# Two constant rows added on GpSimd: b2 into x2, be3 into y

## The reference

```python
xp = L_norm @ h                              # 512 x 512, one matrix for all batches
x1 = relu(layernorm(xp @ Wc + bc, g1, be1)) + h
q, k, v = x1 @ Wq, x1 @ Wk, x1 @ Wv          # 4 heads of 32 features
attn = softmax(where(adj > 0, q k^T / sqrt(32), -1e9))
x2 = layernorm(x1 + (attn v) @ Wo + bo, g2, be2)
m = gelu(x2 @ W1 + b1) @ W2 + b2             # the perceptron, 256 hidden features
out = y + layernorm(x2 + m, g3, be3)
```

## Time and profile before

| what | value |
|---|---|
| median of 3 runs | 990.91 us (985.94 to 995.35) |
| the profiled execution | 985.9 us, of it 984.1 us from the first to the last instruction (the span) |
| mean granted TensorE clock | 0.977 |
| PE busy | 910.1 us (92%) in 7110 instructions |
| DVE busy | 613.4 us (62%) |
| ACT busy | 532.6 us (54%) |
| POOL busy | 328.3 us (33%) |
| one full attention round | about 26.4 us |
| after the rounds (915 us to the end) | 69 us |

### The profile page before, as it was taken

One profiled execution on the slowest core, in us unless ns is written; L12 is line 12 of the kernel. 1 busy time (PEld: TensorE's weight loads), 2 busy tenths in 40 slices (PEclk: granted clock), 3 DMA queues, 4 the chain that ended last, 5 costly groups with the idle time before them and its releaser, 6 DMA issues.

```text
span 984.1 us, 20134 instructions
## 1 busy us (share of the span) xinstructions
PE 910.1 (92%) x7110; PEld 748.6 (76%) x7110; DVE 613.4 (62%) x2009; ACT 532.6 (54%) x1178; POOL 328.3 (33%) x426
## 2 busy tenths in 40 slices
PE   5979899999999999989699999999999999888993
PEld 4848799999999999978467777777777777666782
DVE  5842233333333333634588988988888888886786
ACT  3222222222222333220688888888888888885574
POOL 3110011111111111213335545555444544323776
PEclk9988899999999999999799999999999999999998
DMA  3000000000000000004354444455555454410122
GB/s 94 0 1 12 12 11 12 11 11 11 11 11 11 11 11 11 12 1 122 91 130 109 118 108 116 115 129 130 130 131 130 130 127 119 113 32 1 44 65 65
DMA packets 47218, 61.54 MB, mean 63 GB/s; under 512 B 4377, under 2 KB 22050, under 8 KB 47138
## 3 DMA queue, kind: packets, MB, share of 16 engines
q1 hardware_dynamic: 46034, 60.38, 24.1%
q10 hardware_dynamic: 1104, 0.13, 0.1%
HBM read 39.53 MB, written 20.97 MB: 61 GB/s over the span
## 4 chain that ended last, share of the span: by engine, by line
PE 17%; DVE 10%; issue 9%; POOL 9%; ACT 7%; DVEq 0%; POOLq 0%; ACTq 0%
PE bank L1594 5%; PE bank L1614 3%; DVE prob L1764 3%; PE bank L1658 2%; ACT prob L1705 2%; PE bank L1581 2%; POOL z_gain L301 2%; POOL z_norm L305 2%; POOL rstd_b L186 1%; PE bank L333 1%; PE bank L337 1%; POOL x_bo L1538 1%; DVE z_std L282 1%; POOL rstd L186 1%; ACT prob L1377 1%
## 5 line engine op out<-in xcount | busy, mean ns | idle before, releaser
L1705 ACT ACTIVATE prob<-prob,low 128x512 f32<-128x512 f32 x256 | 183.9, 719 | 51.2 <-DVE low L1764 49.4
L1764 DVE CUSTOM_DVE_ANT_0 prob<-bank,mask 128x512 f32<-128x512 f32 x256 | 171.2, 683 | 26.5 <-PE bank L1581 25.4
L1594 PE MATMUL bank<-ident,prob 128*128 128x128 f32 x1024 | 162.8, 282 | 12.3 <-ACT probT L1694 12.2
L1594 PEld LDWEIGHTS bank<-ident,prob 128*128 128x128 f32 x1024 | 114.7, 141 | 58.1 <-issue 30.3
L1581 PE MATMUL bank<-k_stack,q_stack 128*128 128x512 f32 x256 | 123.7, 485 | 8.8 <-PEq L548 4.9
L811 PE MATMUL bank<-B_hi,T_all 128*128 128x384 f32 x384 | 102.3, 340 | 4.6 <-DVE y L1211 2.6
L1694 ACT ACTIVATE probT<-bank 128x512 f32<-128x512 f32 x176 | 102.4, 582 | 3.3 <-PE bank L1594 1.6
L1097 DVE TENSOR_TENSOR T_all<-bank,T_all 128x512 fp32r<-128x512 f32 x48 | 33.0, 687 | 111.6 <-ACT T_all L920 111.6
L920 ACT ACTIVATE T_all<-bank 128x512 fp32r<-128x512 f32 x48 | 28.4, 591 | 134.2 <-PE bank L823 93.1
L926 ACT ACTIVATE Sq<-bank,trace_inv 128x512 fp32r<-128x512 f32 x64 | 43.9, 686 | 93.7 <-PE bank L746 93.7
L593 POOL TENSOR_SCALAR var_eps<-mv 128x4 f32<-128x4 f32 x16 | 3.6, 226 | 257.6 <-DVE mv L1048 257.6
(11 more groups left out here) (244 smaller groups left out, 1865.6 us busy)
## 6 DMA issues: line engine op xcount, KB each, us to landing
k_stack<-bounce_q SPq DMA_DIRECT2D x64, 256.0 KB, 5.1
q_stack<-bounce_k SPq DMA_DIRECT2D x64, 256.0 KB, 7.4
bounce_q<-k_parts SPq DMA_DIRECT2D x16, 512.0 KB, 2.8
bounce_k<-q_parts SPq DMA_DIRECT2D x16, 512.0 KB, 3.1
x_in<-in_x_dram SPq DMA_DIRECT2D x16, 256.0 KB, 2.8
out_dram<-probT SPq DMA_DIRECT2D x16, 256.0 KB, 2.3
y<-in_adj_dram SPq DMA_DIRECT2D x4, 256.0 KB, 4.6
W1s<-in_L_gnn_W_dram SPq DMA_DIRECT2D x1, 128.0 KB, 2.5
```

The lines of the kernel that those rows point to most:

```text
L1594: last = pe.transpose(psum[2 + u % 2][:, mt * P:(mt + 1) * P], prob[u % RING][:, mt * P:(mt + 1) * P], ident[:, :])
L1705: act.activation(prob[u % RING][:, :], prob[u % RING][:, :], ACT.Exp, bias=low[:, u % TURNED:u % TURNED + 1], scale=-1.0, accum_out=row_su ...
L1764: dve.tensor_tensor_reduce(prob[u % RING][:, :], psum[u % 2][:, :], mask[:, u // HEADS, :], 1.0, 3e38, ALU.add, ALU.min, low[:, u % TURNED ...
```

## The change

b2 is no longer added by PE. `add_b2` on POOL adds it to x2 of a batch in place, after PE has transposed that x2 for the hidden layer (the hidden layer must see x2 without b2), and DVE's z3 step, which adds x2 to the product, waits for it. With that `split_b2` on DVE and the 16 `second_bias` products on PE go, and with `second_bias` its wait on the bank, which moves to `second_product`, behind the transposes of batch r + 2 instead of ahead of them. be3 is added to y in place by `add_be3` on POOL at the end of rounds 1 to 16, for batch r - 1, whose h has been taken from y before; `finish` reads y itself. `scales_3` loses its addition.

```diff
@@ PE
-    def second_bias(pe, b):
-        pe.wait_ge(b2_step, 5)
+    def second_product(pe, b):
+        pe.wait_ge(gelu_ready, HT * (b + 1))
         if b == 0:
             pe.wait_ge(oT_ready, BATCH - 1)
         elif b == 1:
             pe.wait_ge(z2_ready, BATCH)
         else:
             pe.wait_ge(z3_ready, b - 1)
-        pe.matmul(psum[6 + b % 2][:, :], ones_parts, b2_parts[:, :, :].rearrange("k t d -> k (t d)"),
-                  start=True, stop=False, skip_group_check=True)
-
-    def second_product(pe, b):
-        pe.wait_ge(gelu_ready, HT * (b + 1))
         for t in range(NT):
             for j in range(HT):
                 last = pe.matmul(psum[6 + b % 2][:, t * D:(t + 1) * D],
                                  gelu[b % 2][j][:, t * P:(t + 1) * P], W2s[:, j, :],
-                                 start=False, stop=j == HT - 1, skip_group_check=True)
+                                 start=j == 0, stop=j == HT - 1)
         last.then_inc(mlp_psum, 1)
...
         if r < BATCH:
             first_product(pe, r)
-        if r >= 1:
-            second_bias(pe, r - 1)
         if r + 2 < BATCH:
             transpose(pe, r + 2)
         if r >= 1:
             second_product(pe, r - 1)
@@ DVE
     def z3_moments(dve, b):
         dve.wait_ge(mlp_psum, b + 1)
         at_least(dve, z3_std_ready, b - 1)
+        dve.wait_ge(x2_b2_ready, b + 1)
+        dve.sem_inc(dve_waited, 1)
         dve.tensor_tensor(out=z3[b % 2][:, :], in0=psum[6 + b % 2][:, :], in1=x2[:, b * N:(b + 1) * N],
                           op=ALU.add).then_inc(z3_ready, 1)
...
-        dve.tensor_tensor(out=result[b % 2][:, :, :], in0=z3_gain[:, :, :], in1=y_be3[b % 2][:, :, :],
+        dve.tensor_tensor(out=result[b % 2][:, :, :], in0=z3_gain[:, :, :], in1=y[:, b * N:(b + 1) * N].rearrange("p (t d) -> p t d", d=D),
                           op=ALU.add).then_inc(result_ready, 1)
...
-                        if (r, u) == AT_SPLIT_B2:
-                            split_b2(dve)
@@ POOL
     def scales_3(pool, b):
-        if b == 0:
-            pool.wait_ge(o_psum, NT * BATCH)
-        at_least(pool, result_ready, b - 1)
-        pool.tensor_tensor(out=y_be3[b % 2][:, :, :], in0=y[:, b * N:(b + 1) * N].rearrange("p (t d) -> p t d", d=D),
-                           in1=all_tiles(one, BE3), op=ALU.add).then_inc(y_be3_ready, 1)
         inverse_root(pool, b, mv3[b % 2], mv3_ready, ve3, rstd3[b % 2], pool3, z3_std_ready, b - 1,
                      exponent, pool_waited)
...
+    def add_b2(pool, b):
+        pool.wait_ge(x2T_psum, b + 1)
+        own = x2[:, b * N:(b + 1) * N].rearrange("p (t d) -> p t d", d=D)
+        pool.tensor_tensor(out=own, in0=own, in1=all_tiles(one, B2), op=ALU.add).then_inc(x2_b2_ready, 1)
+
+    def add_be3(pool, b):
+        pool.wait_ge(one.h_ready, NT * (b + 1))
+        own = y[:, b * N:(b + 1) * N].rearrange("p (t d) -> p t d", d=D)
+        pool.tensor_tensor(out=own, in0=own, in1=all_tiles(one, BE3), op=ALU.add).then_inc(y_be3_ready, 1)
...
                     if within(r, 0, BATCH - 2):
                         norm_z(pool, one, r + 1)
+                    if r <= BATCH:
+                        add_be3(pool, r - 1)
                 add_bo(0, 0)
                 unrolled(round_, BATCH + 2, first=1)
+                for b in range(2):
+                    add_b2(pool, b)
                 scales_3(pool, 0)
                 round_(BATCH + 2, 0, BATCH // 2 + 1)
+                add_b2(pool, 2)
                 for b in range(1, BATCH):
                     scales_3(pool, b)
+                    if b + 2 < BATCH:
+                        add_b2(pool, b + 2)
```

More of the change, by code:

```diff
@@ L1258 @@
 AT_HIDDEN = ((BATCH + 1, 2), (BATCH + 1, 5))
-AT_W1_LO, AT_SPLIT_B2 = (BATCH, 5), (BATCH, 13)
+AT_W1_LO = (BATCH, 5)
 AT_X2T_LO = ((BATCH, 8), (BATCH, 11), (BATCH + 1, 3), (BATCH + 1, 8), (BATCH + 2, 3))
@@ L1477, in layer1 @@
         z3, z3_std = prob[0:2], prob[2:4]
-        y_be3, result, z3_gain = probT[0:2], probT[2:4], probT[4]
+        result, z3_gain = probT[2:4], probT[4]
         stats3, mv3 = sb("stats3", [P, NT, 6]), [sb(f"mv3{i}", [P, NT, 2]) for i in range(2)]
@@ L1481, in layer1 @@
         rstd3, shift3 = ([sb(f"{n}{i}", [P, NT]) for i in range(2)] for n in ("rstd3", "shift3"))
[L1482 to L1485, removed]
+        x2_b2_ready, y_be3_ready, stats3_ready, mv3_ready, pool3, scales3, z3_std_ready, z3_gain_ready, result_ready = (
+            sem(n) for n in ("x2_b2_ready", "y_be3_ready", "stats3_ready", "mv3_ready", "pool3", "scales3",
                              "z3_std_ready", "z3_gain_ready", "result_ready"))
```

## The result

| | before | changed |
|---|---|---|
| median of 15 runs each | 987.84 us | 996.55 us |
| ratio, 95% interval | | 1.0088 [1.0059, 1.0117] |
| L314, median | 1.06 us | 1.75 us |
| one attention round | 26.38 us | 27.07 us |

The account below looks back on a forecast made before the run. The prediction took chains of waits to bound the kernel, in the rounds a loop through all engines, afterwards a second loop. Its terms, 9.4 - 2.8 + 1.0 = +7.6 us on the median 990.91, gave 998.5 us, range 987 to 1004.

Parts of the forecast that it names:

- The loop bounds the rounds: Attention rounds: a chain of waits through all engines, once a round, sets the time; what lengthens a link lengthens the round.
- the absorbed case: Rival, rounds: PE's 1.22 us a round without work could take up the 0.67 us delay; 989.1 us, chance 0.12.
- The residual waits for the whole POOL operation: Rounds: DVE's residual stands still until add_be3 is nearly over, 0.67 us longer in 14 rounds, +9.4 us.
- The split of b2: Round 16: without DVE's split, transposes come 1.9 us earlier and another 0.9 with no clock drop, together -2.8 us.
- z3 of batch 0 waits for add_b2: Perceptron start: z3 of batch 0 comes 1.87 us later, of which 1.0 is left at batch 1's z3, +1.0 us.
- b2 in the steady turns: Perceptron: one POOL addition of 1.28 us a batch replaces the old one, with 2.6 us of cover; 0.
- if the cover went, DVE would wait for POOL: Perceptron, steady turns: what would follow if the 2.6 us of cover ahead of z3 were lost.
- The sum: Whole kernel: 9.4 - 2.8 + 1.0 = +7.6 us, giving 998.5 us.
- the residual gets the port first: Rival, rounds: the residual starts before add_be3 and takes 0.68 us, gaining 0.38 a round; 983.8 us, chance 0.07.
- The shared port: Rival, rounds: both share the port at half speed, residual at most 1.36 us, term 4.2; 993.3 us, chance 0.06.
- The clock fell: Rival, perceptron: PE waits and its clock falls, six pairs of batches losing 0.5 us each, +3; 1001.5 us, chance 0.10.

Follow-up runs that it names:

- e1: Changed kernel with be3's addition moved within the round from behind z_norm to behind split_h, where POOL idles; ratio to the kernel before 0.9971.
- e4: Changed kernel with be3's addition cut into two instructions of 128x256 in the same place; ratio to the kernel before 0.9996.
- e5: Kernel before with one more wait on POOL, so that rinv in rounds 2 to 15 follows the residual; ratio to the kernel before 0.9939.
- e8: Kernel before with the split of b2 on DVE moved from unit 13 of round 16 to unit 1 of round 17; ratio 0.9971.
- e7: Changed kernel with add_b2 of batches 0 and 1 ahead of round 17 on POOL and of batch 2 ahead of round 18; ratio to before 1.0011.
- e3: Changed kernel with be3 added in scales_3 into its own buffer as before, so the b2 part alone; ratio to the kernel before 1.0113.
- e6: Changed kernel with rinv behind the residual, be3's addition behind split_h and add_b2 of batches 0 to 2 earlier; 977.09 us, ratio to before 0.9873.

## Why the prediction held

- **The loop bounds the rounds.** Held. 0.69 us more in the residual made 0.69 us more in the round (e1, e4, e5 give the same with 0, 0.13 and -0.36). No slack took any of it up, as the absorbed case had needed.
- **The residual waits for the whole POOL operation: +9.4 us.** Held: L314 at 1.75 us against 1.73 foreseen, a round 0.69 longer against 0.67. That holds for 13 of the 14 residuals; that of batch 2 started later within the addition and took 1.36 us, 0.30 more. Together +9.3 us, against the 9.4 of the term. The Trainium skill's rule that the first to start keeps the port for its whole instruction ("SBUF — State Buffer", "Who interferes with whom") agrees with e4 and e5. Its "Summary: rules for kernel authors" says of such a pair "Schedule whichever is off the critical path"; e5 did so with rinv and gained 0.36 us a round.
- **The split of b2: -2.8 us.** Held: -2.88 in e8, and the sum below comes out with it.
- **z3 of batch 0 waits for add_b2: of 1.87 us later 1.0 is left.** The wait was right: the last residual to z3(0) would be 58.49 + 0.67 - 2.8 + 1.87 = 58.2, and is 58.26. This term was mis-sized: z3(0) to z3(1) shrank by 0.17, from 5.73 to 5.56, where 0.87 was foreseen, so 1.7 of the 1.87 is left. The product started 2.85 us behind z3(0), just as worked out; but I kept 1.99 us from there to z3(1) while I let PE idle before it, and it took 2.71. e7 has the same product at full clock in 2.21: 0.5 of the missing 0.7 us is the clock, the other 0.2 is not. I used this effect for the split and did not look for it where the change made a new idle time.
- **b2 in the steady turns: 0.** Held: 8.86 us a pair, and the extra semaphore instruction did not show. The sentence "if the cover went, DVE would wait for POOL" is not how it went in e3: there the root came late, since POOL had two additions ahead of it.
- **The sum.** By the terms as measured, 9.3 - 2.8 + 1.7 = +8.2 us, which is what the stretches give; forecast +7.6, timed +8.7 (5.8 to 11.6). That 998.5 lies 2.0 us from 996.55 is partly luck, since the kernel before itself came out 3.1 us lower than in the three runs that the forecast started from.
- **The rivals.** That the residual gets the port first did not happen by itself; e5 made it happen, and it is worth what was worked out, 0.36 us a round. The shared port would have held L314 at 1.36 us or less and is refuted by its 1.75, and by e4. The clock fell twice between z3(0) and the last microseconds of the changed kernel, for 3.4 us each at 923.3 and 937.0, once in the kernel before (at 922.0). The first fall is the 0.5 us above; the pairs behind the second kept their 8.86 us.

What stays open: the ratios of e6 and e7 lie some 3 to 5 us below what their stretches add up to, and the +0.97 us from the residual of batch 1 to that of batch 2 lies in a stretch where the granted clock was 0.89 in the changed kernel and 0.92 in the other.

## What to carry to other kernels

Before an elementwise operation is put on GpSimd, look which VectorE operations with two SBUF inputs can start while it runs: the later one waits, and the trace books that as its duration and names someone else in the chain. A wait ahead of the GpSimd operation, or cutting it in two, gives the port back; adding an operation where GpSimd idles and VectorE starts no such operation costs nothing, but look at the first rounds too, where the order differs (e1). Where a change makes TensorE idle in a dense stretch (1.72 and 2.74 us here), cost what follows at the lower clock too, as a chance and not as a certainty.

## What the runs showed of the hardware

- The scatter of the runs goes with the granted clock. Of the 29 runs of the kernel before that were timed beside e5 to e8, the fastest, 982.23 us, has a mean of 0.980 and the slowest, 995.72, one of 0.966. The first 440 us are the same code in both kernels, but in windows (columns as in the earlier trace rows) the kernel before had

```profile
25.00:440.00 415.00, 401.91 (x2390) 361.92 (x2389) 157.76 (x568) 114.41 (x209) 54.11 (x90) 0.98 0.03 9
```

and the changed one

```profile
25.00:440.00 415.00, 402.53 (x2342) 361.69 (x2341) 153.87 (x554) 113.56 (x208) 52.12 (x88) 0.95 0.03 9
```

In the same time it executed 48 matmuls less. The first residual started between 445.7 us (e6) and 455.4 (e8) in the ten profiles, with no changed instruction ahead of it. Why the clock was lower in one execution than in another no run shows.
- An idle time of TensorE in the dense stretches was followed by the low clock mostly, not always. Behind the 1.72 us at the split it fell in three of three profiles, at the 2.7 us before the second product of batch 1 in four of four. Some 16 to 20 us behind z3(0), where nine profiles idle 1.8 to 4.9 us, it fell in six and stayed at 1.00 in e1 (2.90 us), e5 (1.85) and e7 (2.46).
- The wait for the port ends 0.13 to 0.15 us before the other's recorded end, in either direction: rinv behind the residual takes 1.07 us (0.61 alone), beginning 0.14 before the residual's end.
- A VectorE operation that reads PSUM and SBUF did not wait: the mask at 809.64 in the changed kernel took 0.67 us beside a POOL subtraction that started at 809.62, z3 of batch 0 in e7 0.69 us beside POOL's x2.
- When both start within about 0.01 us, either can win. Just ahead of round 1, where no experiment changed anything, DVE's L_lo (2.29 us alone) and POOL's h_lo (1.27 alone) start together in all ten profiles. Timeline of the kernel before, then of the changed one:

```profile
474.36 3.42 POOL L1523 TENSOR_TENSOR h_lo<-h,h_hi 128x512 fp32r<-128x512 f32 x1
474.36 2.29 DVE L1823 TENSOR_TENSOR L_lo<-adjT,L_hi 128x2048 fp32r<-128x2048 f32 x1 [6.04 <-ACT L_hi L1738]
```

```profile
479.97 1.26 POOL L1507 TENSOR_TENSOR h_lo<-h,h_hi 128x512 fp32r<-128x512 f32 x1
479.98 3.40 DVE L1812 TENSOR_TENSOR L_lo<-adjT,L_hi 128x2048 fp32r<-128x2048 f32 x1 [6.05 <-ACT L_hi L1729]
```

In eight profiles POOL waits, in the changed kernel and e8 DVE does, and there the next residual comes 30.1 us behind the first instead of 29.0. That is 1 us of difference between executions of the same instructions.
